# Six attention layers of one kernel: from a loop over layers to one unrolled run of all pairs

## The reference

```python
def shift_tokens(t):                     # second half of the features comes from the token before
    a, s = jnp.split(t, 2, -1)
    s = jnp.pad(s, ((0, 0), (1, 0), (0, 0)))[:, :-1]
    return jnp.concatenate([a, s], -1)
...
for i in range(DEPTH):                                                   # DEPTH = 6
    x = attn_layer(shift_tokens(x), Wqkv[i], q_scale[i], k_scale[i], Wo[i]) + x
    x = ffn_layer(shift_tokens(x), ln_g[i], ln_b[i], W1[i], b1[i], W2[i], b2[i]) + x
```

## Time and profile before

| what | value |
|---|---|
| median of three runs | 6717.09 us |
| the profiled execution's own time | 6710.32 us |
| its span, first to last instruction | 6708.7 us |
| mean granted TensorE clock | 0.897 |
| busy, share of the span | PE 81%, DVE 60%, ACT 41%, POOL 35% |
| code fetched (queue of kind instruction) | 592 packets, 9.70 MB |

### The profile page before, as it was taken

The page is one execution under the profiler, slowest core; times in us unless marked ns, Lnnn a source line. Parts: engine busy times, 40 slices in busy tenths (PEclk is TensorE's granted clock), DMA queues, the critical chain, the costliest instruction groups (busy, mean ns, idle before and its releaser), DMA issues. The chain is left out here.

```text
span 6708.7 us, 170083 instructions
## 1 busy us (share of the span) xinstructions
PE 5428.8 (81%) x71376; PEld 3446.5 (51%) x71376; DVE 4042.0 (60%) x6293; ACT 2769.9 (41%) x5040; POOL 2348.5 (35%) x2148
## 2 busy tenths in 40 slices
PE   6877868686777868887888788888888788878884
PEld 4755748484665744443544444444444344434442
DVE  6465655556465656664666466656666566656662
ACT  3133231313233225553555455544554455445552
POOL 2232222222232234442444254425443444434440
PEclk8887878787787879998999899999999899989997
DMA  0000000000000012222222122222222222212221
GB/s 17 4 1 4 1 4 1 4 2 2 4 1 4 1 51 60 54 54 59 56 58 55 51 63 54 54 57 64 54 54 63 57 54 54 66 48 54 54 54 55
DMA packets 242251, 252.83 MB, mean 38 GB/s; under 512 B 28448, under 2 KB 238496, under 8 KB 238752
## 3 DMA queue, kind: packets, MB, share of 16 engines
q1 hardware_dynamic: 241440, 241.34, 14.0%
HBM read 32.65 MB, written 4.19 MB: 5 GB/s over the span
## 5 line engine op out<-in xcount | busy, mean ns | idle before, releaser
L1210 POOL TENSOR_TENSOR turn<-prod 128x512 f32<-128x512 f32 x768 | 977.6, 1273 | 2092.6 <-DVE prod L1248 1224.6
L956 PE MATMUL banks<-w2s,xs 128*128 128x512 f32 x2304 | 1284.9, 643 | 144.3 <-DVE xs L1274 107.1
L1248 DVE TENSOR_TENSOR prod<-banks,tabs 128x1024 f32<-128x1024 f32 x768 | 937.2, 1220 | 171.5 <-ACT sq L1097 170.3
L1219 POOL TENSOR_TENSOR turn<-turn,rs 128x512 f32<-128x512 f32 x768 | 784.5, 1043 | 355.0 <-ACT rs L1114 352.7
L1097 ACT ACTIVATE sq<-banks 128x512 f32<-128x512 f32 x768 | 458.4, 597 | 911.0 <-PE banks L956 910.8
L581 POOL TENSOR_TENSOR ao<-at,msk 128x512 f32<-128x512 f32 x288 | 391.6, 1371 | 1009.6 <-PE banks L358 527.4
L986 PEld LDWEIGHTS banks<-msk,turn 128*128 128x128 f32 x3072 | 347.6, 142 | 533.0 <-issue 518.5
L956 PEld LDWEIGHTS banks<-w2s,xs 128*128 128x128 f32 x2304 | 379.4, 200 | 343.5 <-DVE xs L1274 118.5
L1259 DVE TENSOR_REDUCE ss<-sq 128x8 f32<-128x512 f32 x768 | 519.6, 677 | 1.3
L1033 PE MATMUL banks<-ot,w2s 128*128 128x512 f32 x768 | 411.4, 618 | 132.4 <-DVE y L1304 111.9
L986 PE MATMUL banks<-msk,turn 128*128 128x128 f32 x3072 | 481.0, 280 | 9.3 <-ACT ot L1142 9.3
(11 more groups left out here) (202 smaller groups left out, 9730.4 us busy)
## 6 DMA issues: line engine op xcount, KB each, us to landing
v<-v_tok SPq DMA_DIRECT2D x1152, 132.0 KB
v<-v_tok SPq DMA_DIRECT2D x384, 66.0 KB
v<-v SPq DMA_DIRECT2D x168, 132.0 KB, 2.7
w2s<-in_weights SPq DMA_DIRECT2D x7, 1664.0 KB, 6.9
tabs<-in_rot SPq DMA_DIRECT2D x7, 1024.0 KB, 8.9
w2s<-in_weights SPq DMA_DIRECT2D x6, 1049.5 KB, 5.2
xin<-in_x SPq DMA_DIRECT2D x8, 256.0 KB, 3.6
x_dram<-x SPq DMA_DIRECT2D x8, 256.0 KB, 2.5
```

What stands on the lines that cost most here:

```text
L956: pe.matmul(a_bank(use), xs[:, t % 2, b * P:(b + 1) * P], w[:, at:at + 512], start=True, stop=True).then_inc(a_done, 1)
L1210: gp.tensor_tensor(turn[:, r % ROTS, :, :].rearrange(halves, s=2), prod[:, r % 2, 0, :, :].rearrange(halves, s=2), prod[:, r % 2, 1, :, :] ...
L1219: gp.tensor_tensor(turn[:, r % ROTS, :, :], turn[:, r % ROTS, :, :], along(rs[:, q % 2, b, :], DH), ALU.mult).then_inc(rot_done, 1)
L1248: v.tensor_tensor(prod[:, r % 2, :, :, :], a_bank(use).rearrange("p (h d) -> p h d", h=HU).unsqueeze(1) .to_broadcast([P, 2, HU, DH]), tab ...
```

## The change

The loop over layers, the barrier at its end and the clearing of semaphores between layers are gone. All six layers are one program: 96 units, 384 pairs, 398 steps, 48 tiles counted through, where t % NT is the place in y, tabs and kmask. All counts of semaphores run on. The next layer's first projections stand in the steps of the last pairs.

- The table scaling (before: once per layer, all 2048 columns) is done once in the start block for layer 0, and then by scale_table(t), 256 columns, at the end of step 8t + 11 for tile t of the next layer, 40 times. SP loads each fresh tile of tabs (128 KB) behind the V pieces of unit 2t + 3.
- The weights come in pieces, all from SP: columns of K, Q and V for one half of the heads (768 KB) behind the V pieces of each of a layer's last two units; W_O in two halves (256 KB each) at the new layer's units 0 and 1; W_1 (341 KB) and W_2 with the vectors (196 KB) at its unit 2, behind the old layer's last write of y; the scales for the layer after (128 KB) at unit 2.
- PE, ACT and DVE wait for the piece they need at the first use in a layer, and shifted_in(t) waits for the write of the same tile in the layer before.
- keep_keys sets zeros at a layer's first two units where it copies at the others; SP now also moves V there.
- The start block loads all columns of layer 0.

The core of the diff:

```diff
-UNITS = 2 * NT
+UNITS = 2 * NT * DEPTH
+TILES = NT * DEPTH
+LU = 2 * NT
...
-                sp.dma_start(tabs[:], rot).then_inc(w_loaded, 16)
-                sp.dma_start(w[:, 0:W_1], weights[0, :, 0:W_1]).then_inc(w_loaded, 16)
-                sp.wait_ge(w_loaded, 32)
+                sp.dma_start(tabs[:], rot).then_inc(w_init, 16)
+                sp.dma_start(w[:], weights[0]).then_inc(w_init, 16)
+                sp.wait_ge(w_init, 48)
...
+                v.wait_ge(w_init, 48)
                 v.tensor_copy(kmask[:].rearrange("p t n -> p (t n)"), sq[:, 0, :]).then_inc(init_ready, 1)
-                v.wait_ge(init_ready, 2)
+                v.tensor_tensor(tabs[:].rearrange("p t i d -> p t (i d)"),
+                                tabs[:].rearrange("p t i d -> p t (i d)"),
+                                over_batches(w[:, W_S:W_S + 4 * DH], NT), ALU.mult).then_inc(init_ready, 1)
+                v.wait_ge(init_ready, 3)
...
-        def layer_program(layer):
+        def heads_cols(ap, h):
+            return ap[:, 0:3 * INNER].rearrange("p (k h n) -> p k h n", k=3, h=2)[:, :, h, :]
+
+        def all_layers():
             with nc.Block(no_gpsimd_drain=True) as block:
                 @block.sync
                 def _(sp):
-                    sp.dma_start(w[:, W_1:], weights[bass.ds(layer, 1), :, W_1:].rearrange("l p n -> p (l n)"))\
-                        .then_inc(w_loaded, 16)
                     for U in range(UNITS):
-                        h, t = U % 2, U // 2
-                        if t:
+                        h, layer, u = U % 2, U // LU, U % LU
+                        if U >= 2:
...
+                        if layer + 1 < DEPTH and u >= LU - 2:
+                            sp.wait_ge(a_done, item_use(U, 11) + 1)
+                            sp.dma_start(heads_cols(w, h), heads_cols(weights[layer + 1], h)).then_inc(wq_loaded, 16)
+                        if layer and u == 0:
+                            sp.wait_ge(o_done, NP2 * NT * layer - 4)
+                            sp.dma_start(w[:, W_O:W_O + 4 * P], weights[layer, :, W_O:W_O + 4 * P])\
+                                .then_inc(wo_loaded, 16)
+                        if layer and u == 1:
+                            sp.wait_ge(o_done, NP2 * NT * layer)
+                            sp.dma_start(w[:, W_O + 4 * P:W_2], weights[layer, :, W_O + 4 * P:W_2])\
+                                .then_inc(wo_loaded, 16)
+                        if layer and u == 2:
+                            n = a_use["c", NT * layer - 1, "down"]
+                            sp.wait_ge(a_free[n % 2], n // 2 + 1)
+                            sp.dma_start(w[:, W_1:W_O], weights[layer, :, W_1:W_O]).then_inc(w1_loaded, 16)
+                            sp.dma_start(w[:, W_2:], weights[layer, :, W_2:]).then_inc(w1_loaded, 16)
+                        if layer + 1 < DEPTH and u == 2:
+                            if layer:
+                                sp.wait_ge(tab_ready, NT * layer)
+                            sp.dma_start(w[:, W_S:W_1], weights[layer + 1, :, W_S:W_1]).then_inc(ws_loaded, 16)
+                        if U >= 3 and u % 2 and (U - 3) // 2 < TILES - NT:
+                            t = (U - 3) // 2
+                            sp.wait_ge(red_done, 16 * (t + 1))
+                            sp.dma_start(tabs[:, t % NT, :, :], rot[:, t % NT, :, :]).then_inc(tab_loaded, 16)
+                    sp.wait_ge(vd0, VDMA * UNITS // 2)
+                    sp.wait_ge(vd1, VDMA * UNITS // 2)
...
+                            if U >= LU and U % LU < 2:
+                                pe.wait_ge(wq_loaded, 32 * (U // LU - 1) + 16 * (U % LU + 1))
...
+                        layer, i = g // (NP2 * NT), g % (NP2 * NT)
+                        if layer and i in (0, 4):
+                            pe.wait_ge(wo_loaded, 32 * (layer - 1) + 16 * (i // 4 + 1))
...
+                            if t >= NT and t % NT == 0:
+                                pe.wait_ge(w1_loaded, 32 * (t // NT))
...
+                        if i == 0 and t >= NT:
+                            v.wait_ge(tab_ready, t - NT + 1)
...
-                                        tabs[:, t, which, :].unsqueeze(2).to_broadcast([P, 2, HU, DH]),
+                                        tabs[:, t % NT, which, :].unsqueeze(2).to_broadcast([P, 2, HU, DH]),
...
-                        v.tensor_copy(kx[:, h * UP:(h + 1) * UP, :, 0:WIN],
-                                      kx[:, h * UP:(h + 1) * UP, :, P:KX]).then_inc(kept, 1)
+                        front = kx[:, h * UP:(h + 1) * UP, :, 0:WIN]
+                        if U % LU < 2:
+                            v.memset(front, 0.0).then_inc(kept, 1)
+                        else:
+                            v.tensor_copy(front, kx[:, h * UP:(h + 1) * UP, :, P:KX]).then_inc(kept, 1)
...
+                        half, at = P // 2, t % NT * P
+                        if t >= NT:
+                            n = a_use["c", t - NT, "down"]
+                            v.wait_ge(a_free[n % 2], n // 2 + 1)
...
+                    def scale_table(t):
+                        v.wait_ge(ws_loaded, 16 * (t // NT + 1))
+                        v.wait_ge(tab_loaded, 16 * (t + 1))
+                        tile = tabs[:, t % NT, :, :].rearrange("p i d -> p (i d)")
+                        v.tensor_tensor(tile, tile, w[:, W_S:W_1], ALU.mult).then_inc(tab_ready, 1)
...
-                            if t:
+                            if t % NT:
...
-                    v.tensor_tensor(tabs[:].rearrange("p t i d -> p t (i d)"),
-                                    tabs[:].rearrange("p t i d -> p t (i d)"),
-                                    over_batches(w[:, W_S:W_S + 4 * DH], NT), ALU.mult).then_inc(tab_ready, 1)
                     shifted_in(0)
-                    v.wait_ge(tab_ready, 1)
...
+                        if g % 8 == 3 and 0 <= g // 8 - 1 < TILES - NT:
+                            scale_table(g // 8 - 1)
+            nc.all_engine_barrier(sems_to_clear=range(wq_loaded.num, xm_done.num + 1))
+
+        all_layers()
```

More of the change, by code:

```diff
@@ L834, in local_layers @@
         hid = msk[:, M_OFF:M_OFF + FC * NB, :].rearrange("p (i b) n -> p i (b n)", b=NB)
-        w_init, w_loaded, next_loaded, init_ready = names("w_init", "w_loaded", "next_loaded", "init_ready")
+        w_init, init_ready = names("w_init", "init_ready")
+        wq_loaded, wo_loaded, w1_loaded, ws_loaded, tab_loaded = names(
+            "wq_loaded", "wo_loaded", "w1_loaded", "ws_loaded", "tab_loaded")
         (tab_ready, xs_ready, a_done, a_free0, a_free1, sq_done, red_done, ln_done, stat_done,
@@ L926, in _ @@
                                                  src[(m - 1) * WIN:(m + 1) * WIN, :, :]).then_inc(vd[h], 16)
[L927 to L933, removed]
@@ L938, in _ @@
+                    sp.wait_ge(vd0, VDMA * UNITS // 2)
+                    sp.wait_ge(vd1, VDMA * UNITS // 2)
+                    sp.wait_ge(v_moved, 32 * (UNITS - 2))
+                    sp.wait_ge(wq_loaded, 32 * (DEPTH - 1))
+                    sp.wait_ge(wo_loaded, 32 * (DEPTH - 1))
+                    sp.wait_ge(w1_loaded, 32 * (DEPTH - 1))
+                    sp.wait_ge(ws_loaded, 16 * (DEPTH - 1))
+                    sp.wait_ge(tab_loaded, 16 * (TILES - NT))
                 @block.tensor
@@ L965, in scores @@
                             pe.matmul(blocks(sc[:, h, :]), idb[:],
-                                      kmask[:, t:t + 1, :].to_broadcast([P, NB, 2 * WIN]),
+                                      kmask[:, t % NT:t % NT + 1, :].to_broadcast([P, NB, 2 * WIN]),
                                       start=True, stop=False, skip_group_check=True)
@@ L1164, in ffn @@
                         elif k == 4:
-                            if t == 0:
-                                a.wait_ge(w_loaded, 16)
+                            if t >= NT and t % NT == 0:
+                                a.wait_ge(w1_loaded, 32 * (t // NT))
                             a.wait_ge(xn_ready, t + 1)
@@ L1264, in keep_keys @@
                         v.wait_ge(scores_ready, 4 * (U - 1))
-                        v.tensor_copy(kx[:, h * UP:(h + 1) * UP, :, 0:WIN],
-                                      kx[:, h * UP:(h + 1) * UP, :, P:KX]).then_inc(kept, 1)
+                        front = kx[:, h * UP:(h + 1) * UP, :, 0:WIN]
[3 more added lines that the diff above has]
+                            v.tensor_copy(front, kx[:, h * UP:(h + 1) * UP, :, P:KX]).then_inc(kept, 1)
                     def shifted_in(t):
-                        half, at = P // 2, t * P
+                        half, at = P // 2, t % NT * P
+                        if t >= NT:
+                            n = a_use["c", t - NT, "down"]
+                            v.wait_ge(a_free[n % 2], n // 2 + 1)
                         if t >= 2:
@@ L1318, in ffn @@
                             v.wait_ge(xm_done, t + 1)
-                            if t == 0:
```

(10 more changed lines are left out.)

12 lines of the change are left out of this document (3 added, 9 removed).

## The result

| | us | ratio to before, 95% interval |
|---|---|---|
| before, median of four | 6719.0 | |
| after, median of four (6594.0 to 6607.9) | 6596.9 | 0.9822 [0.9806, 0.9839] |
| forecast | 6527 (6490 to 6590) | 0.9717 |
| after, profiled execution (before: 6710.3) | 6594.1 | |

What follows compares the result with a forecast made beforehand. PE's nearly full in-order stream was taken to bound full-pipeline tiles, with drains between layers. Terms -198.1, +10 and -2 gave -190 us: 6527 against the median (6520 profiled), range 6490 to 6590.

Steps and rivals of the forecast that it cites:

- Removed drains: Between layers: five drain-and-refill stretches of 1023.2 us become ten ordinary tiles of 82.5 us, -198.1 us.
- The tile's own length: Length of each local-layer tile, counted 46 times: kept at 82.5 us, the mean of all 36; called the largest unknown.
- The main term: The five stretches between layers turned into ordinary tiles: -198.1 us.
- Late tiles throughout: Rival: the long run settles into its last tile's 83.1 us, saving 170.8 less 8, total 6554 us; 13%.
- the full 40 us of load breaks: Upper bound for the new weight loads breaking PE's score bursts: 4.0 us for each of two large loads, five times.
- Short tiles throughout: Rival: all tiles take 81.6 us as breaks shrink without the loop, saving 239.8 less 8, total 6485 us; 8%.
- Weights in a full pipeline: Weight loads arriving mid-run, none late, but breaking PE's score bursts: +10 us, bounds nothing to 40.
- Table scaling and loads: 40 scalings on DVE, covered by its wait for scores, and 40 table loads issued by SP, landing in time: cost 0.
- The rival on the slower side: Tables land after their due time and DVE stands 40 times; a 25 us landing gives 6819 us; 2%.
- the half-kept seam: Rival: late weights or held-up V pieces drain PE at each seam, keeping half of 39.6 us: 6626 us; 9%.
- The signs to look for: Profile checks, including seam tiles of 82 to 84 us; wrong if the mean tile leaves 81.6 to 83.2.

Runs made afterwards that it cites:

- e7: The kernel before without ten of PE's waits a tile that an earlier wait already implies: 6709.2 us, ratio 0.9993.
- e2: The kernel after without ten of PE's waits a tile that an earlier wait implies, so a tile has 2560 instructions: 6513.9 us, ratio 0.9714.
- e3: e2 with 164 more satisfied waits at the head of PE's part of the local layers: 6613.6 us, ratio 0.9865.
- e9: e2 with ten satisfied waits put back at one other place in each tile, 2570 instructions again: 6626.6 us, ratio 0.9847.
- e5: e2 with all loads of weights and scales in the run cut to 16 columns, for its time alone: 6492.1 us, ratio 0.9671.
- e6: The kernel after with all loads of weights and scales in the run cut to 16 columns: 6593.8 us, ratio 0.9820.
- e4: The kernel before with 130 satisfied waits at the head of PE's part of each layer: 6917.6 us (one run).

## Why the prediction was wrong, step by step

- *Removed drains, -198.1 us: right.* With the places of the blocks made regular in both kernels (e7 and e2) the step is worth 187 us with the loads in it, where 190 were forecast for both. In the kernel after itself the stretch around a seam shrank from 204.6 to 168.9 us in the mean, no wait ties a layer to the end of the one before, and the dependencies hold as read.
- *The tile's own length: the step that failed.* "I keep the mean of all 36, 82.5, as the nearest thing to a mean over positions." I had seen that the breaks depend on where in the program a tile stands, and then averaged over places that were no sample: six places in a row, the same six in each layer, out of a cycle of 25.6 tiles. The count that shows it was in reach: PE's instructions in a tile against the 256 of a block. Measured: 84.15, so 1.65 x 46 = 76 us, of which 10 had been put in for the loads. In tiles 1 to 46 the breaks add up to 111.3 us in the kernel after and to 52.3 in e2; these 59 us are most of the 68.5 between the two kernels' tiles. The main term was right in size, and this one decided the miss.
- *Late tiles throughout, 13%:* the nearest rival, and still too low at 83.1. Its reason was wrong too: the length doesn't settle, it comes and goes with the place in the code. With the full 40 us of load breaks on top it made my upper end, 7 us too low; neither of the two happened, so that the result lies no further outside is luck.
- *Short tiles throughout, 8%: did not come.* The new kernel's run has no branch, and the idle time in its bursts grew from 64.5 to 98.3 us. The rule weighed there (the Trainium skill, "Runtime: NRT & Kernel Launch", section Instruction fetch mechanics: crossing a block is mostly hidden) agrees by count and not in a burst. Of the 462 block ends in tiles 1 to 46 most leave no break, but straight-line code, with no branch near, stands still for up to 2.2 us at one in the kernel after, and for 2.3 in e3 and e9.
- *Weights in a full pipeline, +10 us:* the mechanism is there (e5), 26 to 29 us for all beside regular tiles, and 3 us in the seam tiles of the kernel after itself (e6), within its noise. The bounds of 0 to 40 hold it. The page "DMA: Bandwidth & Descriptors" of the Trainium skill, section Queues, rings and completion order, says that each DMA engine takes turns between its queues by whole packets, so a large load shares its engines with the code's: the 26 to 29 us of e5 agree in kind.
- *Table scaling and loads, 0: right.* 40 instructions with no wait in front, each a little longer than estimated (0.415 us against 0.35), tables landing in 2.6 us, and tiles of 81.5 us with them in e2 as without them before. In the kernel after:

```profile
L1343 DVE TENSOR_TENSOR tabs<-tabs,w2s x40: 412/415/418, 2592.2 to 5867.8; 128x256 f32<-128x256 f32 x40
```

```profile
w2s<-in_weights SPq DMA_DIRECT2D x10, 768.0 KB, 4.8
tabs<-in_rot SPq DMA_DIRECT2D x40, 128.0 KB, 2.6
```

- *The rival on the slower side* and *the half-kept seam* did not come about: nothing waits for a table or for weights.
- *The signs to look for:* I had written that the mean tile leaving 81.6 to 83.2 would prove me wrong, and that is what it did.

## What to carry to other kernels

Where an engine issues long bursts of very short instructions, count its instructions in a period of the loop and take them modulo a code block (256 here): if the remainder isn't zero, expect the time of a period to be a wave over many periods, as in this kernel, and don't forecast from the mean of a few. A period of whole blocks was worth 1.1% here for ten waits that another wait implied, over half of the 1.8% that the whole change had brought. Whole blocks alone are not enough: in a dear place (e3) all of it was lost again, so try a few places. Compare two structures of a kernel only after that, since unrolling a loop moves all its code.

## What the runs showed of the hardware that I had not expected

- The end of a code block costs PE up to 2.4 us in a burst of score products and nothing in a burst of value products. The second kind is as dense (24576 products in 333.3 us, against 358.2), and of the 462 block ends in tiles 1 to 46 of the kernel after some 177 fall into it, some 174 into score bursts. All 105 breaks are in score bursts. Why only there stays open.
- The packet of 16384 bytes itself takes 1.1 us in the mean. In the break shown above it begins 0.4 us before the start of PE's last product, and PE goes on 2.35 us after that start. The median from a packet's start to PE's going on, 2.5 us over the 105 breaks, is more than twice the packet's own time.
- A break can cost more than its own length. Tiles 14 and 18 have 2.6 and 3.5 us more of breaks than tile 2 and are 6.2 and 7.1 us longer. TensorE is granted 1.2 GHz for 13.7 us in each of them, in tile 2 for 3.4 (the shares 0.92 and 0.98 in the rows above), and PE is busy 77.7 and 77.4 us with what takes 73.1. These are the extremes: over the 46 tiles, 59 us more of breaks than in e2 go with 68.5 us more of time.
- A satisfied wait on PE, where nothing else holds it, costs about 0.1 us (12.4 us for 130 in e4, 17.4 for 164 in e3), though the trace shows each as 0.051; their starts stand 0.106 apart.
